# Attention score products and causal masks in pieces of 32 output rows

## What is computed

```python
q = q * cos + _rotate_half(q) * sin
k = k * cos + _rotate_half(k) * sin
scores = jnp.einsum('bhqd,bhkd->bhqk', q, k) / math.sqrt(hd)
causal = jnp.triu(jnp.ones((S, S), dtype=bool), k=1)
scores = jnp.where(causal[None, None], -jnp.inf, scores)
attn = jax.nn.softmax(scores, axis=-1)
attn_out = jnp.einsum('bhqk,bhkd->bhqd', attn, v)
```

## Time and profile before

| | |
|---|---|
| time, median of 3 runs | 1737.48 us (1735.87, 1737.56, 1737.48) |
| span of the profiled execution | 1734.1 us |
| the profiled execution's own time | not listed apart; the span is 3.4 us under the median of the runs, 1.8 us under the lowest |
| TensorE products, share of the span | 95% |
| VectorE, ScalarE, GpSimd | 55%, 42%, 39% |
| mean granted TensorE clock | 0.982 of 2.4 GHz |

### The profile page before, as it was taken

The page is one execution under the profiler, slowest core; times in us unless marked ns, Lnnn a source line. Parts: engine busy times, 40 slices in busy tenths (PEclk is TensorE's granted clock), DMA queues, the critical chain, the costliest instruction groups (busy, mean ns, idle before and its releaser), DMA issues.

```text
span 1734.1 us, 40451 instructions
## 1 busy us (share of the span) xinstructions
PE 1652.0 (95%) x17108; PEld 1186.6 (68%) x17108; DVE 952.4 (55%) x1978; ACT 722.2 (42%) x1510; POOL 670.1 (39%) x851
## 2 busy tenths in 40 slices
PE   6589999999999999999999999999999999999998
PEld 3467458864688547884588756886478855787477
DVE  6864657356553656546574565636565365744621
ACT  4433462334632455234633346233552346433441
POOL 5733335343542426324263433524353242733110
PEclk9779999999999999999999999999999999999999
DMA  5110000000000000000000000000000000000000
GB/s 184 51 50 13 1 14 3 1 25 13 3 2 6 20 13 3 2 25 1 14 3 1 25 14 2 3 0 25 13 3 2 13 13 1 4 2 0 1 13 13
DMA packets 20387, 25.77 MB, mean 15 GB/s; under 512 B 1488, under 2 KB 18800, under 8 KB 20208
## 3 DMA queue, kind: packets, MB, share of 16 engines
q1 hardware_dynamic: 19872, 22.13, 4.0%
q0 software_dynamic: 336, 1.05, 0.2%
HBM read 18.98 MB, written 4.19 MB: 13 GB/s over the span
## 4 chain that ended last, share of the span: by engine, by line
PE 78%; DVE 11%; ACT 6%; issue 3%; POOL 1%; DMA 1%; SPq 0%; DVEq 0%; POOLq 0%; ACTq 0%
PE ring L1592 19%; PE ring L1606 18%; PE ring L1752 6%; PE attn_out L1772 5%; PE ring L1578 5%; PE ring L1710 3%; PE ring L1538 3%; PE ring L1732 3%; PE ring L1645 3%; PE ring L1735 2%; PE ring L1530 2%; PE ring L1755 2%; PE ring L1615 2%; DVE x_z_xb L1176 1%; DVE big L1266 1%
## 5 line engine op out<-in xcount | busy, mean ns | idle before, releaser
L1333 DVE TENSOR_REDUCE maxes<-ring 128x2 f32<-128x1024 f32 (+5 forms) x290 | 197.5, 739 | 86.4 <-PE ring L1735 85.6
L757 POOL TENSOR_TENSOR rstd<-mean_var,eps_and_power 128x2 f32<-128x2 f32 x96 | 19.3, 201 | 470.0 <-DVE mean_var L1170 470.0
L1606 PE MATMUL ring<-w_down,big 128*128 128x256 f32 x784 | 175.9, 379 | 0.0
L1606 PEld LDWEIGHTS ring<-w_down,big 128*128 128x128 f32 x784 | 147.3, 190 | 19.6 <-issue 0.4
L809 POOL TENSOR_TENSOR big<-big,decay_blocks 128x256 f32<-128x256 f32 x192 | 141.5, 766 | 40.5 <-issue 35.9
L780 POOL TENSOR_TENSOR mix<-mix,z_t 128x512 f32<-128x512 f32 x80 | 85.7, 1100 | 117.8 <-DVE mix L1222 117.8
L1752 PE MATMUL ring<-big 32*128 32x512 f32 (+3 forms) x1024 | 124.6, 472 | 0.9 <-DVE big L1365 0.9
L1266 DVE TENSOR_TENSOR big<-big,decay_blocks 128x256 f32<-128x256 f32 x192 | 123.8, 671 | 1.0
L1024 ACT ACTIVATE big<-ring,up_bias 128x256 f32<-128x256 f32 x196 | 82.1, 470 | 101.3 <-PE ring L1592 101.3
L1592 PE MATMUL ring<-maxes,w_mlp 128*128 128x256 f32 x512 | 118.2, 385 | 0.0
L1592 PE MATMUL ring<-maxes,w_up 128*128 128x256 f32 x512 | 116.3, 381 | 0.7 <-ACT maxes L957 0.7
(11 more groups left out here) (202 smaller groups left out, 3250.1 us busy)
## 6 DMA issues: line engine op xcount, KB each, us to landing
x_in<-in_x SPq DMA_DIRECT2D x8, 512.0 KB, 3.8
delta<-in_x SPq DMA_DIRECT2D x7, 512.0 KB, 3.9
out<-x_z_xb SPq DMA_DIRECT2D x7, 512.0 KB, 2.9
w_mlp<-in_wm SPq DMA_DIRECT2D x2, 1024.0 KB, 6.3
w_mlp<-in_w_exp_t SPq DMA_DIRECT2D x1, 1028.0 KB, 9.1
v_ones<-in_w_con SPq DMA_DIRECT2D x1, 1024.0 KB, 10.1
w_mlp<-in_low_up SPq DMA_DIRECT2D x1, 1016.0 KB, 5.9
w_attention<-in_low_down SPq DMA_DIRECT2D x1, 1016.0 KB, 8.1
```

Of the source, the lines that this page charges most:

```text
L1333: nc.vector.tensor_reduce(maxes[:, t % 2, qt, 32 * gs[0] + row:32 * gs[-1] + row + 1:32], banks[:, first:last, lo:hi], AX_X, ALU.max).then ...
L1606: ins = mm(ps[:, a * D:(a + 1) * D], gelu(b, tag, m, t)[:, a * P:(a + 1) * P], wd[:, m, :], start=(m == 0), stop=(m == NF - 1))
```

## The change

1. Exponentials' scores (`s_exp`): every product of 128 key columns of weights becomes four of 32. Piece a (a = 0, 32, 64, 96) writes output partitions a to a+31. The loop runs over the pieces outside and the heads inside, so sixteen products of 32 by 32 stand where four of 32 by 128 stood, with the same moving columns each.
2. Both masks: one product with 128 rows and 128 weight columns per head becomes four pieces with 32 rows and 32 columns. Head g's pieces use row group g. A piece covers only the columns in which its 32 rows of the diagonal tile need the mask: 128, 96, 64 and 32 for S, 32, 64, 96 and 128 for E (each for two tiles in round b). `filled` is on the last piece of each head.
3. The 128 by 128 identity leaves the table `masks`; its place is taken by the 32 by 32 identity repeated four times that was there for the mixer. Both mask tables hold a 32-row pattern repeated four times.

The score products of `s_max` stay as they were (32 by 128). The diff:

```diff
@@ tables
-        masks = sb("masks", [P, 3 * P + SMALL * SUB], BF16)
-        identb = masks[:, 0:P]
-        future = masks[:, P:2 * P]
-        future_t = masks[:, 2 * P:3 * P]
-        lmask = masks[:, 3 * P:].rearrange("p (l k) -> p l k", l=SMALL)
+        masks = sb("masks", [P, 2 * P + SMALL * SUB], BF16)
+        future = masks[:, 0:P]
+        future_t = masks[:, P:2 * P]
+        lmask = masks[:, 2 * P:].rearrange("p (l k) -> p l k", l=SMALL)
+        identb = lmask[:, 0, :]
@@ s_max
-                for g in range(HG):
-                    mm(ps[g][:, lo:hi], identb, future.unsqueeze(1).to_broadcast([P, (hi - lo) // P, P]),
-                       start=False, stop=True).then_inc(*filled(("S", t, rnd, g)))
+                for a in range(0, P, SUB):
+                    for g in range(HG):
+                        r, n = slice(32 * g, 32 * g + 32), P - a
+                        ins = mm(ps[g][a:a + SUB, lo:hi].rearrange("p (m k) -> p m k", k=P)[:, :, a:P], identb[r, :],
+                                 future[r, 0:n].unsqueeze(1).to_broadcast([SUB, (hi - lo) // P, n]), start=False, stop=True)
+                        if a + SUB == P:
+                            ins.then_inc(*filled(("S", t, rnd, g)))
@@ s_exp
                 for i, (jt, at) in enumerate(parts):
                     n = T - jt * P
+                    for a in range(0, P, SUB):
+                        for g in range(HG):
+                            r = slice(32 * g, 32 * g + 32)
+                            if i == 0 and a == 0:
+                                ps.append(take(("E", t, rnd, g)))
+                            mm(ps[g][a:a + SUB, at:at + n], kp[r, t, jt * P + a:jt * P + a + SUB], qp[r, t, jt * P:T],
+                               start=(i == 0), stop=False)
+                for a in range(0, P, SUB):
                     for g in range(HG):
-                        r = slice(32 * g, 32 * g + 32)
-                        if i == 0:
-                            ps.append(take(("E", t, rnd, g)))
-                        mm(ps[g][:, at:at + n], kp[r, t, jt * P:(jt + 1) * P], qp[r, t, jt * P:T],
-                           start=(i == 0), stop=False)
-                for g in range(HG):
-                    mm(ps[g][:, 0:hi], identb, future_t.unsqueeze(1).to_broadcast([P, hi // P, P]),
-                       start=False, stop=True).then_inc(*filled(("E", t, rnd, g)))
+                        r, n = slice(32 * g, 32 * g + 32), a + SUB
+                        ins = mm(ps[g][a:a + SUB, 0:hi].rearrange("p (m k) -> p m k", k=P)[:, :, 0:n], identb[r, :],
+                                 future_t[r, P - n:P].unsqueeze(1).to_broadcast([SUB, hi // P, n]), start=False, stop=True)
+                        if a + SUB == P:
+                            ins.then_inc(*filled(("E", t, rnd, g)))
@@ layouts
-    masks = np.concatenate([np.eye(P, dtype=f), np.where(k > j, NEG, 0.0), np.where(j > k, NEG, 0.0)]
+    masks = np.concatenate([np.where(k > low, NEG, 0.0), np.where(low > k - (P - SUB), NEG, 0.0)]
```

## The result

The change makes the kernel slower: 1743.1 us in the median of six runs (1740.99 to 1746.09) against 1737.13 us before (1735.87 to 1738.07), a ratio of 1.0031 with a 95% interval of 1.0018 to 1.0044: a small loss, but clear of the noise. I had forecast 1720. The profiled span grew from 1734.1 to 1740.9 us.

A forecast was written before the change was run, and what follows sets the result against it. TensorE's instruction stream was taken as the bound. Of a raw 39 us, 2.25 us per sequence, 18 over eight, would come off the 1734.1 us span: about 1716, plus 3.4 for the median, 1720 us; range 1702 to 1741.

The forecast's parts named there:

- the price of S b's mask: Maxima's masks in round b: 0.30 us after the scores in place of 0.63, saving 0.33, 32 times.
- 0.13 either way: no change: Exponentials' scores: a shorter first load offsets starting sixteen products in place of four, 0.13 us together before and after.
- Rival 1: Pace of issue: 18 ns a two-pass product, 9 a mask piece, 32 us more, 1751 us in all; chance 0.14.
- the 9 to 10 ns of the earlier trace: Record spacing on column groups, hardly less with fewer columns: would fit a pace of issue, not of the stream.
- the burst of the earlier trace: Four products started within 0.03 us, at most 10 ns apart: spoke for a floor of 35 to 40 ns per part.
- 18 us for the masks: Span gain over eight sequences, 2.25 us each, left of the raw 39 us after waits on banks and exponentials.
- The masks of E: Exponentials' masks: no rest ahead, heads side by side; saves 0.27 us in 64 rounds a and c, 0.43 in 32 rounds b.
- The first bank: Head 0's bank in the exponentials' rounds, awaited by the first exponential: complete 0.05 to 0.07 us earlier, not 0.27.
- the 39 us: Raw saving on TensorE's own stream if nothing waited: 17.3 + 13.8 + 10.6 - 2.5.
- E a and E c before S: Exponentials' rounds a and c: S's last head waits for their first exponential, removing nearly all savings outside turn 3.
- turn 2: Rounds b would bring V b forward 0.76 us, but the fourth exponential comes only 0.07 earlier; 0.5 us kept.
- Rival 4: Pieces of a row group take turns: streaming three times more, 197 us less 18, about 1915 us; chance 0.03.

The follow-up runs named there:

- scores_only: Against the kernel before: only the exponentials' scores in 32-column pieces, in all rounds, both masks whole; median 1745.8 us, +11.1 at equal clock.
- masks_only: Against the kernel before: both masks in 32-row pieces, the exponentials' scores whole; median 1746.4 us, -7.1 at equal clock.
- masks_g: As masks_only, but the exponentials' mask pieces run with heads outside and pieces inside; median 1750.3 us, -8.9 against before at equal clock.
- ac_b_masks: Full change, but exponentials' scores whole in round b and heads outside in the exponentials' masks; median 1737.2 us, -8.0 against before at equal clock.
- g_outer: Full change, but the exponentials' mask pieces run with heads outside and pieces inside; median 1740.3 us, -0.3 against before at equal clock.
- s_only: Against the kernel before: only the maxima's masks in 32-row pieces, exponentials' scores and masks as before; median 1744.2 us, -4.0 at equal clock.
- sb_only: Against the kernel before: only the maxima's masks of round b in pieces; median 1741.1 us, -0.7 at equal clock.
- scores_64: Against the kernel before: only the exponentials' scores in pieces, of 64 key columns, in all rounds; median 1732.5 us, -0.8 at equal clock.
- e_only: Against the kernel before: only the exponentials' scores and masks in pieces, the maxima's masks as before; median 1738.9 us, +4.8 at equal clock.

## Why the prediction was wrong

**The profile's bound and the price of S b's mask: right.** TensorE bound the attention, and a mask of S b went from 0.54 to 0.22 us to the next block, as counted.

**The first step that failed: "0.13 either way: no change" for the exponentials' scores**, with its bound of 0.05 us a round. The starts of the first sixteen products were right: 7.5 ns apart in the mean, where it took 7 from the earlier trace rows. But in round b there are 32 products and then 16 mask pieces, and I priced all of them at the pace of the first four. scores_only measures that term: 11.1 us, three fifths of the forecast gain of 18, in the 32 rounds b. Rival 1 had the pace right: 16.6 ns a two-pass product where it said 18, 8.3 ns a mask piece where it said 9. It had the place wrong, since it laid the pace on every product of all 96 rounds and on the masks of S, and so came to 32 us. I took the 9 to 10 ns of the earlier trace rows and the burst of the earlier trace rows as signs for rival explanations; by theory A they are two paces of the same stream.

**The second step that failed: 18 us for the masks.** With the scores at no change, the whole forecast gain was the masks'. Without the costly scores, masks in pieces are worth 7 to 9 us at equal clock (masks_only, masks_g, ac_b_masks), half of the sum or less. So the forecast would have been too high even if the scores had cost nothing. Part of it is the size on TensorE: I left out that sixteen pieces need 0.05 us to start, and in masks_only a mask of E takes 0.21 us in rounds a and c and 0.26 in b to the next block, where I had 0.15 and 0.20. The rest did not reach the end of the program.

**The masks of E** were to save 0.27 and 0.43 us of a block. Behind 64 records they come at 8.3 ns after a stall. Summed over the span, from the first piece to the next block, E's masks took 39.1 us before, and behind whole scores, in masks_only, they take 23.9. In the change it is 53.3, or 44.7 when a piece counts only from the last score product's start.

**The first bank.** I wrote that it would be full 0.05 to 0.07 us earlier. It was full 0.056 later by the modelled ends and 0.07 by the semaphore, since with pieces outside it needs 13 pieces, and at the slow pace. g_outer prices that at 3.4 us. Even at the fast pace it was 0.05 later by the semaphore (masks_only, 389 ns).

**What was absorbed.** That much of the 39 us would not reach the end was right in kind: s_only, which shortens S b by 9 us, S a by 2.5 and S c by 1.8, gains 4.0 at equal clock, and sb_only, which shortens S b by as much, 0.7. That E a and E c before S would give nearly nothing fits. In turn 2 the forecast kept 0.5 us of the saving. In masks_only, with E b and S b both shorter, nothing of it is left up to E c, which starts 4.82 us after E b and did so after 4.81 before, and 0.2 us up to turn 3's E a (9.90 us after E b, before 10.12). In the change these are 5.06 and 10.16. So of the 0.6 us by which V b waits longer in the change, some 0.35 is the saving absorbed, and 0.25 is the exponentials' later start.

**The clock** stood nowhere in the prediction. For this change it is the small part: 0.9795 against 0.9811, some 2 us of the 5 to 6. In the variants it is up to 20 us and turns their verdicts. Rival 4 fell: sixteen parts stream together. The prediction had quoted the Trainium skill, "TensorE: Matmul & The Clock Gate", Part 3 (Packing small matmuls), for the rule that a weight load overlaps with running matmuls only when its row group differs. The trace disagrees for sixteen parts too, four of which share a row group: their 32 records take the 1.15 us above.

**What is settled and what is not.** The slow pace behind 64 records costs 11.1 us in E b's scores (scores_only, gone in scores_64), the late first bank 3.4 (g_outer), and the clock a little; what the slow pace costs in E's masks alone no run separates. s_only and e_only add up to +0.8 where the change has +3.1, a difference of 2.3 ± 1.0 us that is left unexplained. Why the clock falls is open. It falls when full-array masks are replaced beside whole scores (0.9811 to 0.9693), and goes up when scores are in pieces (0.9833, 0.9848). Replacing E's masks too, with the scores in pieces, left it as it was (e_only 0.9833, scores_only 0.9833). Nor is it the masks alone: g_outer has the same masks as masks_g and 0.9795 where that has 0.9653. In the attentions of sequences 0 to 6 the time in which no product streams (counted from the records' starts to their modelled ends less the 0.16 us by which neighbours overlap) was 54 us before and is 55 in scores_64, 55 in sb_only, 61 in g_outer and 63 in masks_g, while the clocks are 0.9811, 0.9848, 0.9780, 0.9795 and 0.9653: it does not order them either. No run separates what the array does from the time for which it waits.

## What to carry to other kernels

Before splitting products over array parts, count the records that stand one behind the other without a wait, loads and passes included: up to 64 here they started 1.7 ns apart, and behind them 4.2 ns, so a split cost nothing up to that count (and gained nothing at equal clock) and cost time beyond it. Order the pieces so that the bank that someone waits for first is full first, not so that all are full last; and look at when the reader starts, since a block that ends sooner on TensorE need not be reported full sooner. And compare variants of a TensorE-bound kernel at equal granted clock before explaining them: 0.001 of clock was 1.3 us here, as much as many of the effects.

## What the runs showed of the hardware

- The first 64 records in a row start 1.7 ns apart (6.7 ns a two-pass product, 3.3 ns a one-pass one), on sixteen parts as on four. Behind them the next comes after a stall of some 0.19 us and then at 4.2 ns a record (16.6 and 8.3 ns; rounds E a and E b of the change).
- The array rests about 0.09 us at each change of part shape, also from 32*128 to 32*32 (90 ns in the median of each kernel that has it). Between scores and masks of the same shape there is no such rest.
- Semaphore events of four products that start 3.3 or 8.3 ns apart and end together come 34 ns apart (E a of the change and of masks_only, S b).
- The Trainium skill, "TensorE: Matmul & The Clock Gate", section "Architectural detail: the array is 16× 32×32, not 1× 128×128", gives the engine's queue a depth of 64. The runs agree: 64 records were fast (scores_64, E b of masks_only), and the 65th was late (E a of the change), as with 128 (scores_only).
- Kernels whose TensorE is busy for 95% of the span alike were granted mean clocks from 0.9653 (masks_g) to 0.9848 (scores_64). Masks in pieces beside whole scores cost 0.016 of clock in masks_g, 20 us by the slope, more than the 9 us that they saved. What lowers the clock is open.
